# Softmax of a fused attention kernel: eight exponentials per unit on ScalarE, straight from PSUM, in place of one behind a subtraction on VectorE

## The reference

```python
q = jnp.einsum('bsd,hpd->bhsp', x, q_w) + q_b
k = jnp.einsum('bsd,hpd->bhsp', x, k_w) + k_b
v = jnp.einsum('bsd,hpd->bhsp', x, v_w) + v_b
scores = jnp.einsum('bhqp,bhkp->bhqk', q, k) / jnp.sqrt(jnp.float32(P))
attn = jax.nn.softmax(scores, axis=2)
ctx = jnp.einsum('bhqk,bhkp->bqhp', attn, v)
```

## Time and profile before

| | |
|---|---|
| median of three runs | 820.19 us |
| the profiled execution, its own time | 819.61 us |
| its span | 818.0 us |
| PE, weight loads, DVE, ACT, POOL busy | 86%, 81%, 64%, 36%, 35% |
| granted clock, mean | 0.911 |
| attention stage in the span | about 98 to 495 us |

### The profile page before, as it was taken

One profiled execution on the slowest core, in us unless ns is written; L12 is line 12 of the kernel. 1 busy time (PEld: TensorE's weight loads), 2 busy tenths in 40 slices (PEclk: granted clock), 3 DMA queues, 4 the chain that ended last, 5 costly groups with the idle time before them and its releaser, 6 DMA issues.

```text
span 818.0 us, 17190 instructions
## 1 busy us (share of the span) xinstructions
PE 702.8 (86%) x6444; PEld 659.7 (81%) x6444; DVE 524.3 (64%) x1151; ACT 297.3 (36%) x643; POOL 289.0 (35%) x318
## 2 busy tenths in 40 slices
PE   5366999997979989969799776169999999999996
PEld 5365899896868878968788666069999999999995
DVE  5485477884867867858668783436648567476561
ACT  4242554542523425325245221133324334243240
POOL 4387101012030030120200204452665666657615
PEclk9778999998998989979989956569999999999998
DMA  7631000000000000000000001513543454434412
GB/s 228 195 122 46 1 2 2 23 2 16 23 15 17 8 18 23 2 15 15 15 16 2 22 9 29 180 41 95 114 91 87 80 140 88 96 81 85 83 15 27
DMA packets 52626, 44.31 MB, mean 54 GB/s; under 512 B 25465, under 2 KB 46118, under 8 KB 52562
## 3 DMA queue, kind: packets, MB, share of 16 engines
q1 hardware_dynamic: 23090, 31.51, 12.7%
q0 software_dynamic: 29472, 11.90, 9.2%
HBM read 34.06 MB, written 11.43 MB: 56 GB/s over the span
## 4 chain that ended last, share of the span: by engine, by line
PE 52%; issue 27%; POOL 7%; DMA 6%; DVE 6%; ACT 2%; POOLq 1%; DVEq 0%; ACTq 0%
PE shared L1272 8%; PE shared L1274 7%; PE shared L1273 7%; PE pair L1274 7%; PE pair L1272 7%; PE pair L1273 7%; DMA token_rows<-sent 4%; PE pair L1367 2%; PE ct_ps L1377 2%; PE vt_ps L1354 1%; POOL wq_lo L554 1%; DMA qkv<-patches 1%; PE shared L1413 1%; PE ct_ps L1507 1%; POOL prob L587 1%
## 5 line engine op out<-in xcount | busy, mean ns | idle before, releaser
L727 ACT ACTIVATE qkv<-shared,bq_sb 128x276 f32<-128x276 f32 x192 | 93.7, 488 | 128.9 <-PE shared L1274 128.9
L1272 PE MATMUL shared<-xT_hi,wq_hi 128*128 128x276 f32 x384 | 127.0, 331 | 5.2 <-DVE xT_lo L969 2.4
L681 POOL DMA_INDIRECT out<-yrow,held x48 | 101.4, 2112 | 73.8 <-DVE yrow L1234 60.2
L1273 PE MATMUL shared<-xT_lo,wq_hi 128*128 128x276 f32 x384 | 113.5, 296 | 0.0
L1274 PE MATMUL shared<-xT_hi,wq_lo 128*128 128x276 f32 x384 | 113.3, 295 | 0.0
L837 ACT ACTIVATE act_f<-pair 128x348 f32<-128x348 f32 (+1 forms) x128 | 51.8, 457 | 97.3 <-PE pair L1274 97.3
L1272 PEld LDWEIGHTS shared<-xT_hi,wq_hi 128*128 128x128 f32 x384 | 75.0, 195 | 13.5 <-ACT x2T L765 2.6
L1272 PE MATMUL pair<-xe_hi,fc_hi 128*128 128x348 f32 (+1 forms) x256 | 82.7, 323 | 1.1 <-DVE xe_lo L1216 1.1
L1274 PE MATMUL pair<-xe_hi,fc_lo 128*128 128x348 f32 (+1 forms) x256 | 83.1, 325 | 0.0
L1273 PE MATMUL pair<-xe_lo,fc_hi 128*128 128x348 f32 (+1 forms) x256 | 83.0, 324 | 0.0
L664 POOL DMA_INDIRECT held<-token_rows,found_ix x48 | 67.1, 1399 | 26.8 <-issue 26.8
(11 more groups left out here) (170 smaller groups left out, 1735.3 us busy)
## 6 DMA issues: line engine op xcount, KB each, us to landing
raw_fc<-c_fc SPq DMA_DIRECT2D x8, 1024.0 KB
raw_pj<-c_proj SPq DMA_DIRECT2D x8, 1024.0 KB
qkv<-patches SPq DMA_DIRECT2D x9, 384.0 KB, 4.3
qkv<-w_qkv SPq DMA_DIRECT2D x6, 512.0 KB, 6.2
token_rows<-sent POOLq DMA_DIRECT2D x8, 285.7 KB, 7.2
out<-h SPq DMA_DIRECT2D x8, 276.0 KB
patch_rows<-z_row SPq DMA_DIRECT2D x9, 128.0 KB, 1.7
qkv<-w_l SPq DMA_DIRECT2D x1, 1024.0 KB, 7.1
```

What stands on the lines that cost most here:

```text
L681: pool.indirect_dma_start(out, bass.IndirectOffsetOnAxis(ap=xg[p][0:n, t, D:D + 1].bitcast(U32), axis=0), yrow[p][0:n, t, :], None, bounds ...
L727: act.activation(qkv[(st.i + shift) % 2][:, c, :], shared[bank][:, 0:GT], ACT.Identity, bias=bq_sb[:, c:c + 1]).then_inc(s_free[bank], 1)
L1272: pe.matmul(dst, l_hi, r_hi, start=(first and n == 0), stop=False)
L1273: pe.matmul(dst, l_hi, r_lo, start=False, stop=False)
```

## The change

`put_exp` issues one ACTIVATE per head, eight per unit. Each reads its 69 x 69 scores from PSUM, takes minus the scaled maximum as bias from the new buffer `shift_by`, writes its part of `expo`, and gives the sum along the queries through `accum_out` into `zsum`, which is doubled. `take_max` no longer subtracts; after the maximum it multiplies the eight maxima by minus the scale. `weigh_values` no longer sums. ScalarE has two waits more, and PE's scores wait for the exponential instead of the subtraction two units back, because the score bank is now read by the exponential.

```diff
             def put_exp(st, u):
                 n = lambda i: UNITS * i + u + 1
+                p = (u + 1) % 2
                 wait(act, s_sub, st, lambda i: n(i) + 1)
-                e = expo[(u + 1) % 2][:, :, :]
-                act.activation(e, e, ACT.Exp, scale=SCALE).then_inc(s_exp, 1)
+                wait(act, s_ctx, st, lambda i: n(i) - 1)
+                wait(act, s_zi, st, lambda i: n(i) - 1)
+                for h in range(UH):
+                    e, q = h // UP, h % UP
+                    done = act.activation(expo[p][:, h, :], pair[p][0:SEQ, e, q * SEQ:(q + 1) * SEQ], ACT.Exp,
+                                          bias=shift_by[p][:, h:h + 1], scale=SCALE, accum_out=zsum[p][:, h:h + 1])
+                done.then_inc(s_exp, 1)
...
                 dve.tensor_reduce(tp, sc, AX, ALU.max).then_inc(s_top, 1)
                 wait(dve, s_top, st, lambda i: UNITS * i + u + 1)
-                wait(dve, s_ctx, st, lambda i: UNITS * i + u - 1)
-                dve.tensor_tensor(ex, sc, tp.unsqueeze(3).broadcast_to([SEQ, 2, UP, SEQ]), ALU.subtract)\
-                    .then_inc(s_sub, 1)
+                dve.tensor_scalar(shift_by[u % 2][:, :], top[:, :], -SCALE, None, ALU.mult).then_inc(s_sub, 1)
...
                 wait(dve, s_exp, st, lambda i: UNITS * i + u + 1)
-                dve.tensor_reduce(zsum[:, :], expo[u % 2][:, :, :], AX, ALU.add).then_inc(s_zs, 1)
-                wait(dve, s_zs, st, lambda i: UNITS * i + u + 1)
-                dve.reciprocal(zinv[:, :], zsum[:, :]).then_inc(s_zi, 1)
+                dve.reciprocal(zinv[:, :], zsum[u % 2][:, :]).then_inc(s_zi, 1)
...
-                wait(pe, s_sub, st, lambda i: UNITS * i + u - 1)
+                wait(pe, s_exp, st, lambda i: UNITS * i + u - 1)
```

More of the change, by code:

```diff
@@ L287, in program @@
             top = sb("top", [SEQ, UH], F32, smem)
-            zsum = sb("zsum", [SEQ, UH], F32, smem)
+            shift_by = [sb(f"shift_by{i}", [SEQ, UH], F32, smem) for i in range(2)]
+            zsum = [sb(f"zsum{i}", [SEQ, UH], F32, smem) for i in range(2)]
             zinv = sb("zinv", [SEQ, UH], F32, smem)
@@ L338, in program @@
         s_h, s_n_ln, s_xn, s_xT_hi, s_xT_lo = (sem(n) for n in ("s_h", "s_n_ln", "s_xn", "s_xT_hi", "s_xT_lo"))
-        s_vt, s_score, s_top, s_sub, s_exp, s_zs, s_zi, s_val, s_ctx, s_c_hi, s_c_lo = (
-            sem(n) for n in ("s_vt", "s_score", "s_top", "s_sub", "s_exp", "s_zs", "s_zi", "s_val", "s_ctx", "s_c_hi", "s_c_lo"))
+        s_vt, s_score, s_top, s_sub, s_exp, s_zi, s_val, s_ctx, s_c_hi, s_c_lo = (
+            sem(n) for n in ("s_vt", "s_score", "s_top", "s_sub", "s_exp", "s_zi", "s_val", "s_ctx", "s_c_hi", "s_c_lo"))
         s_h2, s_h2_out, s_m_ln, s_x2 = (sem(n) for n in ("s_h2", "s_h2_out", "s_m_ln", "s_x2"))
@@ L977, in take_max @@
                 tp = top[:, :].rearrange("s (e q) -> s e q", e=2)
-                ex = expo[u % 2][:, :, :].rearrange("s (e q) k -> s e q k", e=2)
                 wait(dve, s_score, st, lambda i: UNITS * i + u + 1)
```

## The result

The changed kernel takes 860.09 us (median of 4 runs, 859.25 to 861.93) against 819.85 for the kernel before beside it. The ratio is 1.0496, 95% interval 1.0475 to 1.0516: slower by 40 us. The forecast was 870, range 833 to 915.

What follows compares the result with a forecast made beforehand. PE was taken as dense in the attention stage, its largest waits at group boundaries. Terms 22 (u1 to u7), 8 (table), 10 (boundary), 3 (g0) and 6 (g7) sum to 49, called 50: 819.6 + 50 + 0.6 = 870 us, range 833 to 915.

Steps and rivals of the forecast that it cites:

- X: Time a unit's exponential takes on ScalarE, first head's start to last one's end: 2.7 us taken, against 0.65 before.
- Boundary: From u7 to the next group's u0: the chain to xn starts later, 2.0 us five times, 10 us.
- u1 to u2: Middle groups: evacuations behind the longer exponential end later than PE's second y transpose starts, 1.2 us per group.
- u6 to u7: Middle groups: exponential, context, low part and values end after PE's context stood ready, 0.85 us per group.
- Table, u0 to u1: PE waits for the table addition, which moves later: 7.5 us in g2 to g6 and 0.5 in g1.
- Clock: More idle at boundaries may lengthen the 1.2 GHz stretches: priced 0 to 2 us per boundary, 0 kept.
- u2 to u6: Middle groups' steps between these units: PE stalls of 0.5, 0.5, 0.2 and 0.4 us per group.
- g7: Last of the groups g0 to g7: each unit's cycle loses 1.3 and gains 2.05 us, eight times, 6 us.
- The first: Rival: reading the sum from the accumulator is free, X = 2.0 us, time 835 us; chance 0.19.
- The second: Rival: the read-out doesn't overlap, X = 4.3 us, time 967 us; chance 0.15, including values towards it.
- The third: Rival: VectorE's relief wins, X = 1.3 us, time 814 us, deciding below X = 1.6; chance 0.06.
- The fourth: Rival: PE's slack swallows all of the longer exponential at X = 2.7 us, about 820 us; chance 0.02.

Runs made afterwards that it cites:

- second experiment: The changed kernel without accum_out, so no read-outs, with constants in place of the sums: 830.16 us, ratio 1.0131 to the kernel before.
- first experiment: The changed kernel with one exponential of all eight heads without a bias and the sums left out (constants instead): 805.56 us, ratio 0.9851 to the kernel before.
- third kernel: The changed kernel with the small exponential e_gap issued first in u7: 830.49 us, ratio 1.0123 to the kernel before.
- sixth experiment: The changed kernel with waiting evacuations put between the first and second four heads on ScalarE in u0 to u6: 853.85 us, ratio 1.0407 to the kernel before.
- fifth experiment: The changed kernel with four further heads with read-outs per unit into a scratch buffer: 950.26 us, ratio 1.157 to the kernel before.
- fourth kernel: The kernel before the change with the small exponential e_gap issued first in u7: 791.93 us, ratio 0.9685 to the kernel before.
- eighth: One maximum common to all eight heads, one exponential per unit, sums on VectorE, e_gap first in u7: 790.65 us, ratio 0.9645 to the kernel before.
- tenth: The kernel before the change with e_gap first in u7, once more with five rounds: 790.14 us, ratio 0.9645 to the kernel before.
- eleventh: The common maximum for all eight heads with e_gap first in u7, once more with five rounds: 791.06 us, ratio 0.9639 to the kernel before.

## Why the prediction was right

Direction and main mechanism held, and the size was near (870 said, 860 measured): the longer X on ScalarE's queue costs more than VectorE's relief is worth, and the price grows with X at equal work on VectorE. Part of the agreement is luck, in one term of the sum and in errors that cancel. Point by point:

- *VectorE.* 80 us less busy (83 said), the small multiply 0.168 (0.17 said).
- *X.* 2.47, not 2.7. The read-out is an instruction and overlaps, as chosen; the 0.23 per head without it was 0.20. Between the prediction's own points (2.0 and 835, 2.7 and 870) X = 2.47 gives some 858. The rule of the Trainium skill, "ScalarE: Activation LUTs", section "What ACT_TABLE_LOAD costs" (280 ns and 0.833 ns per element, 93 ns of overlap), gives, as an estimate, heads 0.244 apart. The second experiment has 0.203, with 0.323 for one head against an estimated 0.337. The measurement decides.
- *The other page.* The prediction reads the Trainium skill, "Perfetto Trace Analysis", section "Optimizing Scalar/DVE Operations", as speaking against the change. Its sentence on larger operations is on a saturated engine, which ScalarE at 36% was not. The same section says that where Scalar or Vector aren't saturated but cause bubbles on other engines, breaking up instructions may let work complete sooner. Here it did not: eight heads end 2.47 us after their start, one exponential 0.62 to 0.66, and the values need all eight.
- *Waits.* PE's and ScalarE's added waits cost nothing: the first experiment shows no stretch longer, and the changed kernel's list has no wait of PE at its scores and only the old kind of wait of ScalarE at its exponential, for VectorE.
- *Boundary.* 10 said, 9.6 measured, all of it idle time of PE, 7.5 of it the wait for `xn`. *u1 to u2:* 7.2 said, 5.7. *u6 to u7:* 5.1 said, 4.3. These three and the next are the terms with a timeline of their own behind them, and together are 27 of the 40.
- *Table, u0 to u1.* 8 said, 7.7 measured, but by luck. The 1.51 that PE stands behind the table addition is from g4, the one group of g2 to g6 in which the granted clock is 1.00 there. In the other four PE runs at 0.58 to 0.66 and doesn't wait for it at all; the list has this wait once. After the change PE waits for it five times, 3.1 us in all, and idle time grows by 2.5; the other 5.2 are slower work. So the term was taken from the wrong groups, and the clock, kept at 0, made up for it.
- *Clock.* 0 said, with up to 2 us per boundary left in the range. The 5.2 between u0 and u1 are about 1 us per boundary.
- *u2 to u6.* 9.6 said (3, 3, 1.2 and 2.4), 4.1 measured. At u5 to u6 I had values at 5.3 against 4.9; there was no stall. These slacks came from adding durations, not from a timeline, and were up to 0.4 us too tight.
- *g7.* +0.75 a unit said, 3.0 in seven units measured, 0.43 each. With X lower by 0.23 the sum gives 0.52.
- *g0* 3 said, 3.7 measured. *Ahead of the stage* nothing said, 3.0 measured. The eight exponentials of the very first unit lie there, but the third kernel, whose code up to that point is the changed one's, starts at 99.7: this is at least partly spread between runs. Open.
- *Rivals.* The first (X = 2.0, 835) comes near the kernel without read-outs: X = 1.75, 830. The second (X = 4.3) fell with the overlap of the read-outs; its slope above 2.7 (6 us per 0.1) was too flat, 7.6 measured. The third, VectorE's relief, exists, 14 us at X = 0.62 in the first experiment, but its condition was not met and was too generous: between 0.62 (806) and 1.75 (830) the kernel's own 820 lies at about X = 1.3 by a straight line, an estimate, and not at 1.6. The fourth, no change, is out.
- *What the sum doesn't tell apart:* I wrote that what matters is what queues behind the exponential. The sixth experiment brought part of that forward and gained 6 us of 40; where the second four heads then came later, their own end became the wait.

## What to carry to other kernels

Before cutting one instruction into eight on an engine that looks half idle, find what ends on it in each stage and work out how long the queue is held: here 1.8 us more per unit on a 36% busy engine cost 54 us (806 to 860), while 80 us of relief on the busier one were worth 14. A wait measured in one group holds for the others only if the granted clock is the same there: where PE ran slower, the wait was hidden. Count a read-out per accumulator. And look down the list of waits first: the largest one here went away by issuing one 0.19 us instruction earlier, for 27 to 30 us, with no arithmetic changed; some 5 us of the 27 came from the clock, which no longer fell after the wait.

## What was not expected of the hardware

- Short ACTIVATEs with a bias that read PSUM (69 x 69) start 0.203 apart while each lasts 0.323 (second experiment): 0.12 of overlap, against 0.10 for an evacuation of 276 elements and the exponential behind it. The read-out of an accumulator lasts 0.204 and adds 0.09.
- Within a run of heads each record grows, from 0.30 to 0.34 over twelve (fifth experiment), at a constant distance of 0.29.
- Where g3 passes to g4, from one pass of the loop to the next, the boundary is 13.2 us in the fourth kernel and 9.0 to 9.3 at all its others, with the same number of matmuls. It is 14.8, 14.5, 13.2 and 12.3 in the third, eighth, tenth and eleventh. In the fourth PE stands 2.28 us of it ahead of its value transposes and waits there for nothing that the profile shows, and the granted clock of the stretch is 0.87. What causes it was not tried.
